# Attention scores in float32: two heads in one 32-row strip of the array, with wider matmuls, and reordered constants

## The reference

```python
xn = _layernorm(x)
q, k, v = split(xn @ w_qkv)                      # 16 heads, hd = 8
scores = einsum('bhqd,bhkd->bhqk', q, k) / sqrt(8.0)
scores = where(causal, scores, finfo.min)        # s = 256
attn = softmax(scores); o = einsum('bhqk,bhkd->bhqd', attn, v)
h = layernorm(xn + o @ w_o)
# then: 8 experts (128 -> 512 -> 128, gelu), the best two for each row, layernorm
```

## Time and profile before

| | us |
|---|---|
| median of 3 runs | 1308.93 (1301.49 to 1309.05) |
| the profiled execution, its time | 1304.4 |
| its span, first to last instruction | 1302.6 |
| TensorE matmuls busy / weight loads busy | 1084.2 / 865.4 |
| VectorE / ScalarE / GpSimd busy | 682.6 / 640.7 / 569.0 |
| mean granted clock of TensorE | 0.908 of 2.4 GHz |

### The profile page before, as it was taken

The page is one execution under the profiler, slowest core; times in us unless marked ns, Lnnn a source line. Parts: engine busy times, 40 slices in busy tenths (PEclk is TensorE's granted clock), DMA queues, the critical chain, the costliest instruction groups (busy, mean ns, idle before and its releaser), DMA issues. The chain is left out here.

```text
span 1302.6 us, 29447 instructions
## 1 busy us (share of the span) xinstructions
PE 1084.2 (83%) x11041; PEld 865.4 (66%) x11041; DVE 682.6 (52%) x2097; ACT 640.7 (49%) x1377; POOL 569.0 (44%) x708
## 2 busy tenths in 40 slices
PE   1788988899988898989989799988989799877570
PEld 0555655677776776867777577767777677776570
DVE  4445555545456664576555664566546654350313
ACT  0033333465656555645656466555546556633340
POOL 1023237222645446444645436454545436635505
PEclk8598888898989999989989899889989889988795
DMA  5085012463555435444545435363454445567661
GB/s 111 3 169 136 10 25 64 149 174 128 160 161 147 137 122 167 151 120 129 150 150 153 128 120 161 121 177 116 122 160 149 132 135 194 174 212 263 209 225 44
DMA packets 116467, 180.98 MB, mean 139 GB/s; under 512 B 12360, under 2 KB 79464, under 8 KB 116328
## 3 DMA queue, kind: packets, MB, share of 16 engines
q1 hardware_dynamic: 108136, 162.32, 43.2%
q0 software_dynamic: 8192, 16.79, 4.2%
HBM read 145.10 MB, written 38.68 MB: 141 GB/s over the span
## 5 line engine op out<-in xcount | busy, mean ns | idle before, releaser
L748 DVE TENSOR_REDUCE part_max<-ps_quad 128x6 f32<-128x768 f32 x256 | 233.1, 952 | 155.9 <-PE ps_quad L417 155.9
L618 ACT ACTIVATE probs<-ps_quad 128x768 f32<-128x768 f32 x256 | 196.0, 809 | 231.4 <-PE ps_quad L443 230.9
L972 POOL TENSOR_SCALAR_AFFINE_SELECT probs<-probs 128x512 f32<-128x512 f32 x256 | 162.2, 644 | 266.0 <-ACT probs L618 261.7
L654 ACT ACTIVATE act<-ps_ring,weights 128x128 f32<-128x128 f32 x736 | 205.3, 378 | 116.4 <-PE ps_ring L537 115.6
L537 PE MATMUL ps_ring<-tile_t,weights 128*128 128x128 f32 x1472 | 207.8, 288 | 23.1 <-DVE tile_y L877 12.9
L546 PE MATMUL ps_ring<-weights,act 128*128 128x128 f32 x1472 | 213.2, 294 | 9.0 <-DVE tile_y L877 5.4
L537 PEld LDWEIGHTS ps_ring<-tile_t,weights 128*128 128x128 f32 x1472 | 186.6, 199 | 39.8 <-issue 36.7
L546 PEld LDWEIGHTS ps_ring<-weights,act 128*128 128x128 f32 x1472 | 191.6, 204 | 30.0 <-issue 19.0
L977 POOL TENSOR_TENSOR rstd<-var_eps,power 128x4 f32<-128x4 f32 x56 | 57.9, 1034 | 275.4 <-DVE var_eps L704 275.4
L439 PE MATMUL ps_quad<-q4s,k 32*128 32x128 f32 x1024 | 100.5, 337 | 68.2 <-DVE part_max L748 68.2
L1030 POOL DMA_INDIRECT picked<-sorted_outputs,place x128 | 123.6, 966 | 76.5 <-issue 76.5
(11 more groups left out here) (130 smaller groups left out, 1371.7 us busy)
## 6 DMA issues: line engine op xcount, KB each, us to landing
weights<-expert_weights SPq DMA_DIRECT2D x184, 578.0 KB, 4.9
tile_rows<-sorted_rows SPq DMA_DIRECT2D x56, 192.0 KB, 5.0
sorted_outputs<-tile_y SPq DMA_DIRECT2D x56, 192.0 KB, 2.2
query_key_parts<-qk SPq DMA_DIRECT2D x32, 256.0 KB, 2.0
k<-query_key_parts SPq DMA_DIRECT2D x64, 64.0 KB
q<-query_key_parts SPq DMA_DIRECT2D x64, 64.0 KB
sorted_rows<-zeros SPq DMA_DIRECT2D x2, 1472.0 KB, 10.8
xs<-in_L_attn_x SPq DMA_DIRECT2D x8, 256.0 KB, 6.7
```

The lines of the kernel that those rows point to most:

```text
L618: sc.activation(probs[:, r % PROBS, 2 * a:2 * a + 2, :], ps_quad[:, 2 * a:2 * a + 2, 0:3 * P], ACT.Exp, scale=HD ** -0.5).then_inc(pair_fr ...
L654: ins = sc.activation(act[:, k % ACTS, f, :], bank(use)[:, f * P:(f + 1) * P], ACT.Gelu_apprx_tanh, bias=weights[:, k % WEIGHTS, 2 * F + f ...
L748: dve.tensor_reduce(part_max[:, :, heads, j].rearrange("p c i -> p i c"), ps_quad[:, heads, 0:3 * P].rearrange("p i (c k) -> p i c k", c=3 ...
L972: pool.affine_select(out=both, in_=both, compare_op=ALU.is_ge, fill=0.0, base=0, pattern=[[0, 2], [0, 2], [1, P]], channel_multiplier=-1). ...
```

## The change

Two heads now share one strip. A strip has 4 shift rows and 2 x 8 head rows (heads 8g + 2s and 8g + 2s + 1 of strip s, group g of 2). The weights of both matmuls (`q_stack`, `k_stack`) hold both heads one under the other. The moving side (`k_apart`, `q_apart`) has a copy for each head b, in which the rows of the other head are zero, so that a matmul of 2 x 256 columns gives both heads apart, and one of 2 x 128 the rest. Unit (n, j) uses strips 2(j mod 2) and 2(j mod 2) + 1. Results stand as 768 columns over a pair of banks; the maxima, exponentials and corner work on as many elements as before. `shift` becomes two instructions (`q_sum` of 512 columns, `q_apart` of 1024), with a new semaphore `q_ready` for TensorE. `spread` is cut into `spread_out` and `spread_in`; keys are read back three times as often (4 DMAs into `k_stack`, 8 into `k_apart`). The columns of the query and key weights are reordered in the kernel (`w_qk`). Constants that are not needed first move behind the first norm (`constants`), and the bias piece behind the first projection. In the diff below, lines that it removes are left out where the functions above show them.

```diff
+STRIPS = 4
+SHIFTS = HEADS // STRIPS
+STACK = 2 * HD
...
-        put(first - 4, "misc_1", ("turn", m))
-        put(first - 4, "misc_2", ("project", m, 1))
-        put(first - 4, "second_c", ("spread", m, 1))
-        put(first - 4, "misc_3", ("project", m, 0))
-        put(first - 4, "end", ("spread", m, 0))
+        put(first - 4, "turn_tiles", ("turn", m))
+        put(first - 4, "misc_1", ("project", m, 1))
+        put(first - 4, "second_b", ("project", m, 0), ("spread_out", m, 1))
+        put(first - 4, "misc_2", ("spread_out", m, 0))
+        put(first - 4, "second_c", ("spread_in", m, 1))
+        put(first - 4, "first_b", ("spread_in", m, 0))
...
+    put(-5, "end", ("constants",))
+    put(-4, "misc_2", ("bias",))
...
+            def spread_out(m, which):
+                freed(sp, ("project", m, which))
+                sp.dma_start(parts[m % 2, which], qk[:, which, :]).then_inc(parts_out[which], 16)
+
+            def spread_in(m, which):
                 rows = parts[m % 2, which]
+                into = (q_stack, k_stack)[which]
+                if m < 2:
+                    sp.wait_ge(strips_set, m + 1)
+                elif which:
+                    pair_used(sp, ("exps", 2 * m - 3, GROUPS - 1), 1)
+                else:
+                    freed(sp, ("shift", 2 * m - 3))
+                sp.wait_ge(parts_out[which], 16 * (m + 1))
+                for i in range(STRIPS):
+                    at = SLOT * i + SHIFTS
+                    sp.dma_start(into[at:at + STACK, m % 2, :, :],
+                                 rows[SLOT * i:SLOT * (i + 1), :].rearrange("(r g) t -> r g t", g=2)
+                                 ).then_inc(parts_in[which][m % 2], 16)
                     if which:
+                        for b in range(2):
+                            given = SLOT * i + STACK * b
+                            sp.dma_start(k_apart[at + HD * b:at + HD * (b + 1), m % 2, :, b, :],
+                                         rows[given:given + STACK, :].rearrange("(d g) t -> d g t", g=2)
+                                         ).then_inc(parts_in[which][m % 2], 16)
...
             def scores(n, j):
                 m, at, par = n // 2, n % 2 * S, n // 2 % 2
                 if j == 0 and n % 2 == 0:
+                    pe.wait_ge(parts_in[0][par], 16 * STRIPS * (m // 2 + 1))
+                    pe.wait_ge(parts_in[1][par], 16 * 3 * STRIPS * (m // 2 + 1))
+                if n == 0 and j == 0:
+                    pe.wait_ge(bf_ready, 1)
                 no = QUAD_NO["scores", n, j]
+                g, first = j // 2, j % 2 * 2
                 for a in range(2):
                     if no:
                         pe.wait_ge(pair_free[a], no)
+                    rows = slice(SLOT * (first + a), SLOT * (first + a + 1))
+                    pe.matmul(ps_quad[:, 2 * a, :], q_stack[rows, par, g, at + P:at + S],
+                              k_apart[rows, par, g, :, at:at + S].rearrange("r b (c k) -> r c b k", c=2),
+                              start=True, stop=True, tile_position=(SLOT * (first + a), 0))
                 for a in range(2):
+                    rows = slice(SLOT * (first + a), SLOT * (first + a + 1))
+                    pe.matmul(ps_quad[:, 2 * a + 1, 0:2 * P], q_stack[rows, par, g, at:at + P],
+                              k_apart[rows, par, g, :, at:at + P], start=True, stop=True,
+                              tile_position=(SLOT * (first + a), 0))
+                for a in range(2):
+                    for to in (ps_quad[:, 2 * a, 2 * P:4 * P], ps_quad[:, 2 * a + 1, 0:2 * P]):
+                        mm = pe.matmul(to, ident_bf[:, :], causal[:, :].unsqueeze(1).broadcast_to([P, 2, P]),
+                                       start=False, stop=True, skip_group_check=True)
                     mm.then_inc(pair_full[a], 1)
...
             def exps(n, j):
                 at, par = n % 2 * S, n // 2 % 2
+                g, first = j // 2, j % 2 * 2
                 if j == 0:
+                    pe.wait_ge(q_ready, n + 1)
                 for a in range(2):
                     pe.wait_ge(pair_free[a], QUAD_NO["exps", n, j])
+                    rows = slice(SLOT * (first + a), SLOT * (first + a + 1))
+                    pe.matmul(ps_quad[:, 2 * a, :], k_stack[rows, par, g, at:at + P],
+                              q_apart[rows, n % 2, g, :, :].rearrange("r b (h q) -> r h b q", h=2),
+                              start=True, stop=True, tile_position=(SLOT * (first + a), 0))
+                for a in range(2):
+                    rows = slice(SLOT * (first + a), SLOT * (first + a + 1))
+                    pe.matmul(ps_quad[:, 2 * a + 1, 0:2 * P], k_stack[rows, par, g, at + P:at + S],
+                              q_apart[rows, n % 2, g, :, P:S], start=True, stop=True,
+                              tile_position=(SLOT * (first + a), 0)).then_inc(pair_full[a], 1)
...
+                    sc.activation(probs[:, r % PROBS, a, :],
+                                  ps_quad[:, 2 * a:2 * a + 2, :].rearrange("p b n -> p (b n)")[:, 0:6 * P], ACT.Exp,
                                   scale=HD ** -0.5).then_inc(pair_free[a], 1)
...
             def scores(n, j):
+                g, first = j // 2, j % 2 * 2
                 for a in range(2):
                     pair_used(dve, ("scores", n, j), a)
+                    banks = ps_quad[:, 2 * a:2 * a + 2, :].rearrange("p b n -> p (b n)")[:, 0:6 * P]
+                    dve.tensor_reduce(part_max[:, :, first + a, 2 * g:2 * g + 2],
+                                      banks.rearrange("p (c b k) -> p c b k", c=3, b=2), AX.X, ALU.max
                                       ).then_inc(pair_free[a], 1)
...
             def shift(n):
                 use = ("shift", n)
                 if n >= 2:
                     pair_used(dve, ("exps", n - 2, GROUPS - 1), 1)
                 full(dve, use)
+                dve.tensor_tensor(q_sum[:, :, :], q_stack[:, n // 2 % 2, :, n % 2 * S:n % 2 * S + S],
+                                  bank(use)[:, 0:S].unsqueeze(1).broadcast_to([P, 2, S]), ALU.add
                                   ).then_inc(free_sem(use), 1)
+                freed(dve, use)
+                dve.tensor_tensor(q_apart[:, n % 2, :, :, :], q_sum[:, :, :].unsqueeze(2).broadcast_to([P, 2, 2, S]),
+                                  head_mask[:, :, :].unsqueeze(3).broadcast_to([P, 2, 2, S]), ALU.mult
+                                  ).then_inc(q_ready, 1)
...
+            def strips(par):
+                dve.memset(q_stack[:, par, :, :], 0.0)
+                dve.memset(k_apart[:, par, :, :, :], 0.0)
+                dve.tensor_scalar(k_stack[:, par, :, :].rearrange("p g t -> p (g t)"),
+                                  shift_rows[:, :].broadcast_to([P, 2 * TOK]), -1.0, None, ALU.mult
+                                  ).then_inc(strips_set, 1)
+
+            def constants():
+                strips(1)
...
+            dve.wait_ge(const_pool, CONSTANTS_POOL)
+            step(dve.tensor_reduce(row_of[:, :], ident[:, :].rearrange("p (a r) -> p r a", r=SLOT), AX.X, ALU.add))
             settle()
+            step(dve.tensor_reduce(shift_rows[:, :], row_of[:, 0:SHIFTS], AX.X, ALU.add))
+            settle()
+            strips(0)
+            dve.wait_ge(w_in, 16)
+            for which in range(2):
+                ins = dve.tensor_copy(w_qk[:, which, :].rearrange("p (r g) -> p r g", g=2),
+                                      w_given[:, which * D:(which + 1) * D].rearrange("p (g r) -> p r g", g=2))
+            ins.then_inc(weights_turned, 1)
```

178 lines of the change are left out of this document (73 added, 105 removed).

## The result

The changed kernel takes 1556.91 us (median, 1553.51 to 1560.24); the kernel before, on the same chip, 1308.46 us (1301.49 to 1309.05). The ratio is 1.191, 95% interval 1.186 to 1.196: slower, by 248 us.

A forecast was written before the change was run, and what follows sets the result against it. TensorE was taken as the bound, though with holes. The terms 179 - 50 + 9 + 0 - 6 + 42 = +174 us on 1304.4 us gave 1478 us, forecast as 1481 us for the runs' median; range 1395 to 1565 us.

The forecast's parts named there:

- the clock falls far: Rival: half-array units count for less, so TensorE's granted clock falls to 0.82 or 0.84, 1591 or 1558 us; chance 20%.
- (1): TensorE's units: 768 columns through each of two strips, 1.52 us a unit for 0.88, +179 us (165 to 200).
- (2): Units' weight loads halved: nothing gained, since loads run under the columns of others; bound -26 us.
- The first rival: Rival: weight loads, not columns, set a unit's time, so halving them makes the kernel faster, 1194 us; chance 3%.
- (3): TensorE's waits: longer units fill holes, smaller waits and pairs that come apart, -50 us (-15 to -110).
- (4): VectorE's shift in two instructions: costs time only in 12 holes where TensorE waits, +9 us (0 to +22).
- (5): SP's 8 more DMAs a chunk for the spread: cost 0, as loads are issued ahead of need; bound +42 us.
- (6): The start: earlier first norm and the two writes together before the reads, -6 us (-9 to +2).
- (7): TensorE's granted clock: falls from 0.92 to 0.89 with half-array units, +42 us (-40 to +200).
- nothing at the units: Rival: one stream feeds all four strips, so units cost the same and only start and shift count, 1307 us; chance 4%.
- the holes take more and the clock rises: Rival: TensorE's waits give back 110 us and units stand at full clock, 1342 us, or 1406 with 80 us; chance 16%.

The follow-up runs named there:

- experiment 1: The kernel before with the odd head of each pair left out of scores and exps, so units use two of four strips: 1347.07 us, ratio 1.028.
- experiment 2: The changed kernel with 256 and 128 columns in place of 512 and 256, each strip's second head left out: 1388.66 us, ratio 1.061.
- experiment 3: The changed kernel with its units' matmuls each cut into two, same columns and strips, twice the weight loads: 1582.75 us, ratio 1.210.
- start-only kernel: The kernel before with the changed kernel's order at the start, and the old units and heads: 1304.20 us, ratio 0.996.
- experiment 8: The start-only kernel with a second VectorE instruction of 512 columns in each shift, its result overwritten: 1323.98 us, ratio 1.011.
- experiment 9: The start-only kernel with 8 more small DMAs a chunk on SP, reading keys back into a spare tile: 1304.49 us, ratio 0.998.
- experiment 6: The start-only kernel: the kernel before with only the changed kernel's order at the start: 1304.20 us, ratio 0.996.
- experiment 4: The changed kernel with added matmuls in the two idle strips, which the unit's 256-column matmuls wait for: 1602.2 us, ratio 1.224.
- experiment 5: The changed kernel with 256-column matmuls waiting for the unit's two 512-column ones, nothing in the idle strips: 1644.59 us, ratio 1.256.

## Why the prediction was right, and where it was not

The sign, the mechanism at the units and the range held (1395 to 1565). The time came out 76 us above the 1481 forecast and 8 us below the upper end, outside the 1430 to 1530 us to which the forecast gave 57%; what came is the rival "the clock falls far", which had 20%. So the range held in part by luck. Its sum has a slip too: 1478 + 4.5 is 1482.5, not 1481.

(1) *Columns per strip*: right. 1.49 us a unit for 1.52. Experiments 1 and 2 show the rest of the claim: two strips take as long as four, and half of the columns bring 0.85 us back.

(2) *Half the loads, 0*: near in size, a little off in its reason. Twice the loads cost 0.13 us a unit (experiment 3), and only in the short matmuls. The first rival is out: the units' loads halved in number, and the unit got longer with its columns.

(3) *Waits filled, -50*: the sum was about right by the estimate above, its parts were not, and that is luck. Busy time rose by some 135 us at full clock and not 165, and gaps gave 18, of which 4 are the start; 30 + 14 is near 50. The wait for the maxima was to fall to 45 us and is 78.9. But the holes did not shrink. The hole of the earlier trace rows was held to be one that TensorE does not start. The changed kernel's timeline of VectorE at such a hole:

```profile
709.05 1.82 DVE L780 TENSOR_REDUCE part_max<-ps_quad 128x6 f32<-128x768 f32 x2 [1.78 <-PE ps_quad L443]
...
711.77 0.86 DVE L728 BATCH_NORM_STATS2 stats<-end_rows 128x6 f32<-128x128 f32 x4
...
722.00 0.69 DVE L946 TENSOR_TENSOR xs<-xs,end_rows 128x512 f32<-128x512 f32 x1 [6.32 <-POOL end_rows L1092]
```

GpSimd's timeline in the same place:

```profile
713.34 1.04 POOL L1029 TENSOR_TENSOR rstd<-var_eps,power 128x4 f32<-128x4 f32 x1 [5.54 <-DVE var_eps L735]
714.58 1.08 POOL L1085 DMA_INDIRECT picked<-sorted_outputs,place  x1 [0.19 <-issue]
...
718.48 0.95 POOL L1085 DMA_INDIRECT picked<-sorted_outputs,place  x1 [0.31 <-issue]
719.44 1.23 POOL L1024 TENSOR_SCALAR_AFFINE_SELECT probs<-probs 128x512 f32<-128x512 f32 x2
720.65 1.25 POOL L1092 TENSOR_TENSOR end_rows<-end_rows,g_half 128x512 f32<-128x512 f32 x1
```

In the changed kernel the chain goes back to TensorE: the maxima wait 1.78 us for its unit, the statistics stand behind them, the power waits 5.54 us for the statistics, and gathers, masks and scaling follow. The hole was 3.77 us for 4.10, not 1.9 shorter. I had stopped at GpSimd's row at 550 and not asked what its power had waited for: in the trace of the kernel before it waits 4.54 us, until 560.72, for VectorE's statistics, and VectorE had waited 4.09 us, until 552.87, for gathered rows. There the chain went back to a gather's landing; with longer units TensorE itself is the late one. The 30 us came from units: I put them to pairs that come apart less often, which is argued from the sum and was not tested.

(4) *The shift, +9*: too small by what an instruction of 0.69 us costs in the start-only kernel, 20 us (experiment 8), near the bound of 22. The step counted only 12 holes as exposed. The product itself took 1.25 us and the sum 0.69. What the two cost in the changed kernel stayed open.

(5) *Spread, 0*: right as far as tested, with half of the bytes (experiment 9).

(6) *Start, -6*: right in sign, 4.1 us at the first scores (31.25 us, where 29 was forecast), 4.8 us in time (experiment 6).

(7) *The clock, +42*: this is the term that was mis-sized. With the 14 us of step (1) the forecast had 56 us for it, and the rows give 134. The mean fell to 0.827 where 0.89 was taken; the case "the clock falls far" put 0.84 at 1558 us, and that is what came. I chose "nearer to unchanged" without a row for it. The low row that I had, 0.79 in the early stretch, was no better a forecast: that stretch itself went to 0.50, below the bound that I built on it, and 0.79 everywhere would have made 1639 us. What I left out is that the clock, once it has fallen behind a hole, stays down longer with these units: the windows behind that hole have 13.5 us at 0.50 where the kernel before has 6.6. The two gaps I left open are now closed: a unit in half of the strips lowers the granted clock (experiment 1), filling them raises it in units with a wait in the same place (experiments 4 and 5), and the number of matmuls is not what does it (experiment 3). (The Trainium skill, TensorE: Matmul & The Clock Gate, Part 1, has the clock follow how busy the array has been lately. If busy means covered by matmuls, the changed kernel disagrees: 38.00 of 38.00 us, at 0.57. The other reading, how much of the array works, agrees with the runs here.)

The rivals: with a unit of 1.49 us, "nothing at the units" is out; "the holes take more and the clock rises" failed on both halves.

## What to carry to other kernels

Packing more into fewer row strips saves loads and costs columns: price a unit by the columns through its fullest strip, not by the number of matmuls. Then ask what share of the array the new form uses, since a TensorE that is busy in half of its strips can lose the clock for everything beside it. Neither the mean clock of the kernel before nor that of its lowest stretch told how far; leaving heads out of the kernel before (experiment 1) showed the direction with a small edit, so measure such a run before giving a price. And follow a wait back through every engine: a queue of gathers on GpSimd looked like the cause and was a link.

## What the runs showed of the hardware

TensorE's granted clock was 0.57 over 38 us that matmuls covered without a gap. A kernel that leaves half of the scores out was 2.8% slower than the one that computes them, and one with additional matmuls in idle strips 42 us faster than the same without. The changed kernel's clock fell 35 times for 31, and stayed down for some 538 us for 240. Twice as many matmuls and weight loads in the same strips did not raise it (0.821 to 0.831). One of the chips ran the kernel before in 1385 us, 5.8% over the others, at nearly the same TensorE clock (0.885 to 0.900, for 0.895 to 0.917).
